# Two stages of a Trainium2 kernel: a flag loaded before the border, four stores that land behind it, one low part computed first, and row sums in four narrow column groups

## The reference, cut to what matters

```python
x = x + attention0(layernorm(x))   # 8 heads of 64, keys and values through a latent of 64
x = x + ffn0(layernorm(x))         # silu(x w1) * (x w2), gelu(. h1), gelu(. h2), . w3; hidden 1024; weights -1, 0, 1 and a scale
x = x + attention1(layernorm(x))   # 16 heads of 16, rotary positions on queries and keys
x = x + ffn1(layernorm(x))         # silu(gate) * up, down; hidden 768; integer weights
# attention: softmax(q k^T / sqrt(d)) v, then the output projection
```

## Time and profile before

| | |
|---|---|
| median of 3 runs | 2463.66 us (2458.45, 2463.93, 2463.66) |
| the profiled execution's own time | 2452.89 us |
| its span, first to last instruction | 2451.1 us |
| TensorE busy | 2352.9 us, 96% of the span |
| VectorE, ScalarE, GpSimd busy | 1508.7, 1352.8, 1044.7 us |
| mean granted TensorE clock | 0.987 |
| first stage | ends at about 801 us |
| second stage | TensorE's first matmul at 811.03 us |

### The profile page before, as it was taken

How to read it: one execution, slowest core, us unless ns; L and a number is a source line. 1 busy time by engine, 2 the same in 40 slices (tenths; PEclk the granted TensorE clock), 3 DMA queues, 4 the chain that set the end, 5 groups by cost and what they waited for, 6 DMA issues and landing times. The chain is left out here.

```text
span 2451.1 us, 38790 instructions
## 1 busy us (share of the span) xinstructions
PE 2352.9 (96%) x15141; PEld 1458.9 (60%) x15141; DVE 1508.7 (62%) x1934; ACT 1352.8 (55%) x1787; POOL 1044.7 (43%) x674
## 2 busy tenths in 40 slices
PE   6989999999999899999999999999999999999899
PEld 4545555555555687877877877544444444444598
DVE  6887777777774223322222222689989989889364
ACT  3555555554454444444444444378878778778643
POOL 1656766766677346556456456130010000000354
PEclk8999999999999999999999999999999999999999
DMA  1211321221212455555555555533432333332232
GB/s 50 71 68 53 96 78 53 96 74 48 73 42 68 139 170 172 170 181 182 175 180 183 169 180 181 148 96 73 90 88 64 89 77 73 90 79 50 61 113 82
DMA packets 157702, 259.02 MB, mean 106 GB/s; under 512 B 37872, under 2 KB 98160, under 8 KB 157168
## 3 DMA queue, kind: packets, MB, share of 16 engines
q1 hardware_dynamic: 157520, 256.53, 34.9%
HBM read 206.52 MB, written 60.68 MB: 109 GB/s over the span
## 5 line engine op out<-in xcount | busy, mean ns | idle before, releaser
L1825 DVE TENSOR_REDUCE m_mraw<-m_R 128x2 f32<-128x1024 f32 x512 | 622.5, 1221 | 70.2 <-PE m_R L126 58.5
L1676 ACT ACTIVATE m_P<-m_R 128x1024 f32<-128x1024 f32 x512 | 524.1, 1025 | 151.6 <-PE m_R L126 151.3
L581 ACT ACTIVATE a_P<-a_S 128x1024 f32<-128x1024 f32 x256 | 248.9, 1024 | 208.3 <-PE a_S L126 208.3
L126 PE MATMUL m_O<-m_P,m_V 128*17 128x256 f32 x4096 | 330.5, 394 | 4.5 <-ACT m_P L1676 2.6
L1930 POOL TENSOR_TENSOR m_act0l<-m_xf,m_act0h 128x512 fp32r<-128x512 f32 x128 | 164.6, 1289 | 240.2 <-ACT m_xf L1738 136.3
L879 POOL TENSOR_TENSOR a_accp<-a_accp,a_P 128x1024 f32<-128x1024 f32 x96 | 250.9, 2614 | 15.2 <-ACT a_P L581 6.4
L126 PE MATMUL a_O<-a_P,a_V 128*64 128x512 f32 x1024 | 247.7, 605 | 4.5 <-ACT a_ON L589 4.5
L126 PE MATMUL m_R<-m_act0h,wt 128*128 128x512 f32 x640 | 251.4, 393 | 0.0
L712 DVE TENSOR_REDUCE a_mraw<-a_X 128x2 f32<-128x1024 f32 x164 | 200.0, 1219 | 82.9 <-PE a_X L126 82.9
L126 PE MATMUL m_R<-m_act0l,wt 128*128 128x512 f32 x640 | 250.4, 391 | 0.0
L126 PE MATMUL m_R<-m_act1h,wt 128*128 128x512 f32 x512 | 203.0, 397 | 12.3 <-POOL m_act1l L1930 12.3
(11 more groups left out here) (244 smaller groups left out, 4264.2 us busy)
## 6 DMA issues: line engine op xcount, KB each, us to landing
wt<-wcopy SPq DMA_DIRECT2D x176, 512.0 KB, 3.4
m_xres<-x SPq DMA_DIRECT2D x96, 128.0 KB, 3.0
m_K<-bounce_k SPq DMA_DIRECT2D x96, 128.0 KB, 5.2
m_ln_x<-x SPq DMA_DIRECT2D x23, 512.0 KB, 4.2
a_tile<-in_L_ffn_tiles SPq DMA_DIRECT2D x22, 512.0 KB, 4.7
wcopy<-in_L_ffn_tiles SPq DMA_DIRECT2D x22, 512.0 KB, 5.4
m_Q<-bounce_q SPq DMA_DIRECT2D x150, 64.0 KB, 2.3
x<-m_xres SPq DMA_DIRECT2D x64, 128.0 KB, 2.7
```

The source lines that it names most:

```text
L126: return pe.eng.matmul(out, lhsT, rhs, start=start, stop=stop, skip_group_check=True)
L581: act.eng.activation(P[n % NP][:, :, :], psS[n % 2][:, :, :], ACT.Exp, scale=SCALE).then_inc(s_exp)
L1676: act.eng.activation(P[h % 4][:, :, :], pair(key)[:, :, :], ACT.Exp, scale=SCALE).then_inc(R.free(key))
L1825: dve.eng.tensor_reduce(mraw[u % 2][:, at, :], pair(key)[:, :, :], AX.X, ALU.max).then_inc(R.free(key))
```

## The change

- TensorE's flag is loaded at the end of the first stage, after the last `sums`, and the second stage only branches on it.
- The stores of `TAIL` count on a semaphore of their own, `s_tail`, which lives beyond the border. SP waits at the end of the first stage for the stores before them alone. The four residual tiles `xres` are shared by both stages; the first loads into them, and the load of the last block's input, wait for `s_tail`.
- `sums` of all units but the last makes four matmuls of 32 columns of weights and 256 columns of data; `total` is 256 wide, `keep_sums` copies 256 columns, and `move_sums` is one DMA.
- On GpSimd the `low` of the tile (0, 7) stands before `rotate`.
- `send_high` and `send_low` stand four half-steps after the projection instead of three, `send` six instead of five; `fill_queries` moves from START + 46 to 48 and `fetch_query(5)` from START + 48 to 50.

```diff
 def sums(u):
-    terms = (accd[u % 2],) if u < NU - 1 else (accd[u % 2], accp)
-    for i, acc in enumerate(terms):
-        for h in range(NH):
-            ins = mm(pe, bank(key)[64 * h:64 * h + 64, :], ones[:, :], acc[:, h, :], i == 0, i == len(terms) - 1)
+    if u < NU - 1:
+        for i in range(4):
+            ins = mm(pe, bank(key)[32 * i:32 * i + 32, 0:256], ones[:, 0:32], accd[u % 2][:, i // 2, 256 * (i % 2):256 * (i % 2) + 256])
+    else:
+        for i, acc in enumerate((accd[u % 2], accp)):
+            for h in range(NH):
+                ins = mm(pe, bank(key)[64 * h:64 * h + 64, :], ones[:, :], acc[:, h, :], i == 0, i == 1)
 def move_sums(u):
-    for h in range(NH):
-        sp.eng.dma_start(rcol[64 * h:64 * h + 64, :], total[64 * h:64 * h + 1, :]).then_inc(s_total, 16)
+    sp.eng.dma_start(rcol[:, :], total[0:128:32, :]).then_inc(s_total, 16)
 def keep_sums(u):
-    act.wait_ge(s_total, 32 * u)
-    act.eng.activation(total[:, :], bank(key), ACT.Copy).then_inc(X.free(key))
+    act.wait_ge(s_total, 16 * u)
+    act.eng.activation(total[:, :], bank(key)[:, 0:256], ACT.Copy).then_inc(X.free(key))
 def store(b, t):
-    sp.eng.dma_start(x_tiles(x_out, b)[:, t, :], xres[i % 4][:, :]).then_inc(s_store[i % 4], 16)
+    landed = shared.s_tail if (b, t) in TAIL else s_store[i % 4]
+    sp.eng.dma_start(x_tiles(x_out, b)[:, t, :], xres[i % 4][:, :]).then_inc(landed, 16)
 # end of the first stage, SP
 for i in range(4):
-    sp.wait_ge(s_store[i], 16 * B * NT // 4)
+    sp.wait_ge(s_store[i], 16 * (B * NT // 4 - 1))
 # end of the first stage, TensorE
 sums(NU - 1)
+pe.wait_ge(s_low, LOWS + 2)
+shared.flag = pe.eng.value_load(inexact[0:1, 0:1])
 # second stage, TensorE
-flag = pe.eng.value_load(inexact[0:1, 0:1])
-with pe.eng.If(flag != 0):
+with pe.eng.If(shared.flag != 0):
 # second stage, SP: load_residual, load_norm
+    else:
+        sp.wait_ge(shared.s_tail, 64)
...
+    elif (which, k) == ("b", NB - 1):
+        sp.wait_ge(shared.s_tail, 64)
 def send_at(H):
-    return x_of(H - 5, "project")
+    return x_of(H - 6, "project")
 def send_high_at(H):
-    return x_of(H - 3, "project")
+    return x_of(H - 4, "project")
 # SP, fetch_query
-if (h + 32) % 16 == 0 and 0 <= (h + 32) // 16 < 6:
+if (h + 32) % 16 == 0 and 0 <= (h + 32) // 16 < 5:
     fetch_query((h + 32) // 16)
+if h == 50:
+    fetch_query(5)
 # second stage, GpSimd
-    if H == START + 46:
+    if H == START + 48:
         fill_queries()
...
+    awaited = [key for key in ended_at(H) if key[0] == "hidden" and key[2:] == (0, MT - 1)]
+    for key in awaited:
+        low(key)
     if x_of(H, "project"):
         rotate(*x_at(H)[1:])
     for key in ended_at(H):
-        if key[0] == "hidden":
+        if key[0] == "hidden" and key not in awaited:
             low(key)
```

More of the change, by code:

```diff
@@ L54, in __init__ @@
         self.wt = [sb(f"wt{i}", [128, 1024], F32R) for i in range(3)]
+        self.xres = [sb(f"xres{i}", [128, 256]) for i in range(4)]
         self.scol, self.s3 = sb("scol", [128, 4, HID0 // 128]), sb("s3", [128, 88])[:, 0:2]
         self.inexact = sb("inexact", [1, 1], I32)
+        self.s_tail = nc.alloc_semaphore("s_tail")
 class Engine:
@@ L364, in attention_a @@
         mrow = [p.sb(f"mrow{i}", [NH * 4, 128], F32R) for i in range(2)]
-        total = p.sb("total", [128, 512])
+        total = p.sb("total", [128, 256])
         wraw = p.sb("wraw", [128, NG, 320])
@@ L369, in attention_a @@
         osp = [[p.sb(f"osp{i}{j}", [128, NG, 128], F32R) for j in "hl"] for i in range(2)]
-        xres = [p.sb(f"xres{i}", [128, 256]) for i in range(4)]
+        xres = shared.xres
         tile, tile_hi, itile = p.sb("tile", [128, 1024]), p.sb("tile_hi", [128, 1024], F32R), p.sb("itile", [128, 1024], I32)
@@ L740, in invert @@
             def invert(u):
-                dve.wait_ge(s_total, 32 * (u + 1))
+                dve.wait_ge(s_total, 16 * (u + 1))
                 dve.eng.reciprocal(rcol[:, :], rcol[:, :]).then_inc(s_rcol)
@@ L1304, in ffn_attention_ffn @@
         p = Place(nc, ctx, "m")
-        ident, identr, inexact = shared.ident, shared.identr, shared.inexact
+        ident, identr = shared.ident, shared.identr
         banks = p.ps("R", [128, 6, 512])
@@ L1336, in ffn_attention_ffn @@
         yt = [p.sb(f"yt{i}", [128, 512]) for i in range(2)]
-        xres = [p.sb(f"xres{i}", [128, 256]) for i in range(XR)]
+        xres = shared.xres + [p.sb(f"xres{i}", [128, 256]) for i in range(4, XR)]
         mraw, mneg = [p.sb(f"mraw{i}", [128, 16, 2]) for i in range(2)], p.sb("mneg", [128, 2, 8], F32R)
```

## The result

The changed kernel takes 2421.48 us (median of four runs, 2418.31 to 2428.58); the kernel before, beside it on the same chip, takes 2462.36 (four runs, 2458.45 to 2463.93). The ratio is 0.984, 95% interval 0.9815 to 0.9865: faster, by 41 us as the medians stand. A second measurement of the same kernel gave 2425.99 us and a ratio of 0.9865 (0.9848 to 0.9882), 32 us as the medians stand. The profiled executions took 2452.89 us before (span 2451.1, granted clock 0.987) and 2418.31 after (span 2416.5, clock 0.990).

The account below looks back on a forecast made before the run. TensorE was taken to bound the first stage's steady part, with low-part gaps in the second and a border pause; 20.3 + 7.6 + 2.0 = 29.9 us off 2463.66 gave 2433.8, say 2434, range 2422 to 2448.

Parts of the forecast that it names:

- Second stage, 20.3 us: Blocks of the second stage: low part before `rotate` removes TensorE's gaps, 12.3 us, and the clock falls behind them, 8.0 us.
- a hole of 1.3: GpSimd at s = 34: `send_low`, behind the fifth low part, waits for ScalarE's `send_high`, taking back 1.3 us.
- First send late: ScalarE at s = 34: `send_high` waits for the first send's landing, at worst 0.4 us late, inside the 0.8 us margin.
- the rival of a landing over 6.0 us: Second stage: a late first send makes `send_high` hold back the awaited tile; a 10.7 us landing gives 2471; chance 0.03.
- TensorE waited for L1839: Second stage, s = 40: TensorE waiting for VectorE's swap of the last projection's bank would show the prediction wrong; no size given.
- Falls of the clock, 8.0 us: Second stage: without gaps, the five falls of TensorE's clock behind them go, 1.60 us each.
- Sums, 7.6 us: First stage: narrow `sums` save 0.28 us net each, counted for 27 of 31; bounds 3.6 to 11.8 us.
- waits for VectorE would swallow some: First stage: shorter sums lengthen TensorE's waits for VectorE's maxima after four of the first five; seven later units may swallow theirs.
- The DMA less is hidden: First stage: one DMA fewer in `move_sums` is hidden behind TensorE and only makes the inverse sums earlier for GpSimd.
- Border, 2.0 us: Between the stages: SP's 1.35 us store wait falls away and the flag's load, 0.6 us, moves to where TensorE stands still.
- the expectation of 7.7 us from VectorE's addition to the first matmul: Border: from VectorE's last addition to the second stage's first matmul, about 7.7 us instead of 9.64.
- the upper bound: Border: gain of 4.8 us if the branch took only the 2.6 us of a transfer's median landing.

## Why the prediction was right, and where it was not

The prediction was 2434 us, range 2422 to 2448, from a sum of 29.9 us. The two measurements give 41 and 33 us; the first median, 2421.48, is half a microsecond below the range, the second, 2425.99, inside it.

- **Second stage, 20.3 us: right, 21.7 and 21.0 measured**, and 21.5 with its two edits alone. The low part ends 0.6 us ahead of TensorE where 0.8 were forecast, GpSimd's wait for the first `send_high` is 0.99 us where a hole of 1.3 was forecast, no clock falls, and a block takes 91.3 us where 91.6 were forecast. The one term left out is small: the first matmul behind a gap took 0.50 or 0.60 us where its neighbours in the changed kernel take 0.39, which over seven gaps makes about 1 us. The forecast had treated the moved sends as a part of the cost; they are what lets the gain through, 11.7 us without them.
- **First send late:** `send_high` waited 0.19 us in the row shown, and the rival of a landing over 6.0 us did not come. That the move could be harmful was right in kind: alone it costs 19.2 us. The sign of being wrong "TensorE waited for L1839" came with the low part alone, where `send_high` still stands at its old place.
- **Falls of the clock, 8.0 us: right in sum**, but they are not tied to the gaps one to one. With one DMA alone, all six 1.91 us gaps are there and three falls; with the sums part alone, the six gaps and four falls. The profile of before, with five, is one draw of these.
- **Sums, 7.6 us: right in what one saves, 0.28 forecast and 0.30 seen in the rows shown, mis-sized in the count.** All 31 narrow sums pay, not 27, at 0.29: 9.0 us, and the stretches without TensorE's waits differ by 9.1. That waits for VectorE would swallow some did not happen. These waits move by up to 7 us between profiles of kernels with the same sums (17.8 and 25.0 us), and their mean is not longer than before: 10.6 us in the means. "The DMA less is hidden" was right (1.0002).
- **Border, 2.0 us: wrong, -0.4 in the first profile and -1.3 in the second.** The step that failed is the expectation of 7.7 us from VectorE's addition to the first matmul; 10.06 and 10.88 were measured. Its two terms were right (1.46 for SP's wait where 1.35 stood, 0.54 for the flag), and the branch, left at 5.41, even gave 1.1 us, toward the upper bound. What was missing is the code's place: 248 instructions more in the first stage moved the branch's target to where a second fetch costs 3.55 us. With the target elsewhere the border takes 6.92 us, a gain of 2.7: 1.2 from SP, 0.5 from the flag and 1.0 from the branch. That is more than the 2.0 of the sum, so the hole alone made the term negative.
- **Start of the span, -1.4, and the tail of the stage, -0.9:** nothing was forecast. The first sum comes at 72.9 to 74.9 us in the fourteen profiles, whatever the edits; why is open. The tail goes with the clock: the fall of the granted clock to 0.50 ahead of the border lasts 3.4 us in eight profiles, and there last sum to last matmul takes 13.6 or 13.7 us; it lasts 6.8 us in the six others, and there it takes 14.3 to 14.5. The edits don't decide which.

So the median came out under the forecast by 12.5 us in the first measurement and by 8 in the second, although a term of 2 us turned negative. The second stage explains 0.7 to 1.4 and the sums 1.4 to 3, and the border takes 2.4 to 3.3 back. That the second measurement's 32 us lie so near the 29.9 is in part luck, since the surplus of two terms and the loss at the border cancel. The rest I can't put on a step: the kernel before also stood at 2455.6 to 2458.3 in the later measurements, so part of it is the spread between measurements.

## What to carry to other kernels

Where an in-order queue holds back a critical operation, moving that operation up is only half an edit: what it was moved past is now late, and whoever waits for that must move as well (11.7 us with one half, a loss of 19.2 with the other, a gain of 21.5 with both). Measure a part by itself before believing a surplus in one profile: 5 us of "gain" here was the same kernel's difference between two profiles. Taking the waits out of a stretch showed what the edit was worth in each profile by itself. And ahead of a far branch, any change in the number of instructions can open or close a hole of some 4 us; compare the first instructions behind the branch in both traces.

## What was unexpected of the hardware

- TensorE's branch to its other list took 4.25 to 5.75 us. In eight of fourteen profiles 3.5 to 5.5 us more passed behind one load of weights, until another packet of 16.4 KB of code had come. Adding 48 instructions ahead of the branch removed this second part, adding 256 brought it back.
- The same branch takes 1.1 us less if the register it compares was loaded long before (4.25 to 4.43 against 5.33 to 5.75 us). The packet of code that it waits for also starts sooner behind the branch's start, 1.0 to 2.0 us instead of 2.9 to 3.3; why is not shown.
- An addition of 128x1024 on VectorE beside one of GpSimd's, at the same place of the same unit, took 2.91 to 3.15 us in the five profiles with wide sums and 1.48 to 2.06 in the nine with narrow ones.
